# Pairwise dots of a DLRM tower: one wide matmul for four samples, against four narrow ones on their own array columns

## The reference

```python
e = jnp.stack([tbl_0[ids[:, 0]], ..., tbl_26[ids[:, 26]]], axis=1)   # (2048, 27, 128)
dot = jnp.einsum('bnd,bmd->bnm', e, e)
z = dot.reshape(2048, 27 * 27)[:, idx]          # the 351 pairs i < j
h = jnp.concatenate([z, dense_ctx], axis=1)     # 351 + 16 columns
h = jnp.maximum(h @ W_top1 + b_top1, 0.0)       # 367 -> 512
h = jnp.maximum(h @ W_top2 + b_top2, 0.0)       # 512 -> 256
y = h @ W_top3                                  # 256 -> 1
```

## Time and profile before

| | us |
|---|---|
| median of 2 runs | 441.38 |
| the two runs | 442.3 and 440.45 |
| span of the profiled execution | 599.8 |

### The profile page before, as it was taken

How to read it: one execution, slowest core, us unless ns; L and a number is a source line. 1 busy time by engine, 2 the same in 40 slices (tenths; PEclk the granted TensorE clock), 3 DMA queues, 4 the chain that set the end, 5 groups by cost and what they waited for, 6 DMA issues and landing times.

```text
span 599.8 us, 8311 instructions
## 1 busy us (share of the span) xinstructions
PE 416.3 (69%) x2864; PEld 391.5 (65%) x2864; DVE 263.6 (44%) x723; ACT 169.1 (28%) x296; POOL 291.1 (49%) x311
## 2 busy tenths in 40 slices
PE   2130749647876887689766986598768966998607
PEld 2120648647876876688666985597768856998506
DVE  5210745354636444435427462563536453642302
ACT  2110304213323242223223332243323231444201
POOL 6775543645665456545664566545655656000000
PEclk9755667768878998779976987699769987998957
DMA  7941211211341133212431234113321333012230
GB/s 199 248 124 44 68 44 49 80 36 54 96 128 43 37 99 102 79 32 75 99 106 29 70 84 120 43 28 98 102 76 35 92 95 96 4 49 59 50 38 11
DMA packets 58896, 45.29 MB, mean 76 GB/s; under 512 B 39972, under 2 KB 52644, under 8 KB 58876
## 3 DMA queue, kind: packets, MB, share of 16 engines
q1 hardware_dynamic: 49148, 25.09, 16.6%
q0 software_dynamic: 9728, 19.94, 12.4%
HBM read 37.92 MB, written 7.09 MB: 75 GB/s over the span
## 4 chain that ended last, share of the span: by engine, by line
PE 37%; another core or an unknown queue 31%; issue 9%; DVE 9%; DMA 8%; ACT 4%; SPq 1%; ACTq 0%; DVEq 0%
PE dots_ps L605 12%; PE onehot_ps L581 6%; DMA dots_dram<-dots 6%; DVE mask L486 6%; PE onehot_ps L583 6%; PE tile_ps L594 4%; PE mlp_ps L614 3%; PE mlp_ps L616 3%; PE mlp_ps L615 3%; ACT emb L366 2%; DVE dots L204 2%; ACT dots L204 1%; DVE tab_lo L505 1%; DMA emb<-tbl 1%
## 5 line engine op out<-in xcount | busy, mean ns | idle before, releaser
L344 POOL DMA_INDIRECT rows<-tbl,idx x304 | 290.4, 955 | 218.1 <-issue 102.8
L581 PE MATMUL onehot_ps<-mask,tab_hi 125*128 125x256 f32 x512 | 159.5, 338 | 85.0 <-DVE mask L486 43.3
L486 DVE TENSOR_SCALAR mask<-idb,cmp 125x256 fp32r<-125x256 int32 x512 | 155.4, 372 | 85.7 <-remote 59.0
L581 PEld LDWEIGHTS onehot_ps<-mask,tab_hi 125*128 125x128 f32 x512 | 119.2, 233 | 91.1 <-issue 62.7
L605 PE MATMUL dots_ps<-emb 128*128 128x108 f32 x1024 | 145.3, 300 | 30.7 <-ACT emb L366 20.3
L605 PEld LDWEIGHTS dots_ps<-emb 128*128 128x128 f32 x1024 | 138.5, 215 | 38.6 <-issue 26.9
L204 DVE COPY dots<-dots_ps 32x216 f32<-32x216 f32 x128 | 66.8, 522 | 207.9 <-remote 127.8
L583 PE MATMUL onehot_ps<-mask,tab_lo 125*128 125x256 f32 x512 | 151.1, 321 | 2.0 <-issue 2.0
L583 PEld LDWEIGHTS onehot_ps<-mask,tab_lo 125*128 125x128 f32 x512 | 119.4, 233 | 0.8 <-issue 0.7
L204 ACT COPY dots<-dots_ps 32x216 f32<-32x216 f32 x128 | 67.1, 524 | 165.3 <-remote 88.7
L594 PE MATMUL tile_ps<-ident,rows 128*128 128x128 f32 x304 | 56.7, 313 | 37.0 <-ACT emb L366 27.2
(11 more groups left out here) (32 smaller groups left out, 150.2 us busy)
## 6 DMA issues: line engine op xcount, KB each, us to landing
idb<-ids_onehot SPq DMA_DIRECT2D x16, 512.0 KB
dots_dram<-dots SPq DMA_DIRECT2D x7, 864.0 KB
rows<-tbl,idx POOLq DMA_INDIRECT x304
emb<-tbl SPq DMA_DIRECT2D x8, 448.0 KB
zT<-dots_dram SPq DMA_DIRECT2D x16, 117.0 KB
idb<-ids_onehot SPq DMA_DIRECT2D x8, 128.0 KB, 4.3
zT<-dots_dram SPq DMA_DIRECT2D x8, 104.0 KB
dots_dram<-dots SPq DMA_DIRECT2D x1, 540.0 KB
```

What stands on the lines that cost most here:

```text
L344: nc.gpsimd.indirect_dma_start(rows[:, q, r, :], None, tables[GATHERED[r]][:, :], bass.IndirectOffsetOnAxis(idx[:, k, r:r + 1], 0)).then_i ...
L486: made = nc.vector.tensor_scalar(mask[0:VP, h, c, :], idb[0:VP, f, :], cmp[0:VP, at:at + 1], None, ALU.is_equal)
L581: nc.tensor.matmul(out, tab_hi[0:VP, f, at, :], mask[0:VP, h, c, :], start=(at == 0), stop=False)
```

## The change

For each sample of a quad there is now a matmul of its own: 32 columns of weights (the sample's), 27 columns streamed, with the output on the 32 partitions of that sample, which puts it on its own 32 columns of the array. All 8 quads of a unit lie side by side in one bank (8 x 27 = 216 columns). Each engine then empties its two samples, which are 64 neighbouring partitions, in one copy.

```diff
 def empty_dots(copy, engine, b, parity, u, samples, empty):
     engine.wait_ge(dots_ps_full, UNITS * b + u + 1)
-    for s in samples:
-        a, z = PAD * s, PAD * (s + 1)
-        src = dots_ps[a:z, u % 2, :, 0:QUADS_BANK * QUAD * FEATURES].rearrange(
-            "p a (c t j) -> p a c t j", c=QUADS_BANK, t=QUAD)[:, :, :, s, :]
-        dst = dots[a:z, parity, :, u * UNIT_Q:(u + 1) * UNIT_Q].rearrange(
-            "p j (a c) -> p a c j", a=UNIT_BANKS)
-        taken = copy(dst, src)
-    taken.then_inc(empty, 1)
+    a, z = PAD * samples[0], PAD * (samples[-1] + 1)
+    copy(dots[a:z, parity, :, u * UNIT_Q:(u + 1) * UNIT_Q],
+         dots_ps[a:z, u % 2, 0, 0:UNIT_Q * FEATURES].rearrange("p (c j) -> p j c", c=UNIT_Q)
+         ).then_inc(empty, 1)
...
 def dot_unit(b, parity, u):
...
     for i in range(UNIT_Q):
-        at = (u * UNIT_Q + i) * QUAD
-        col = i % QUADS_BANK * QUAD * FEATURES
-        done = nc.tensor.matmul(
-            dots_ps[:, u % 2, i // QUADS_BANK, col:col + QUAD * FEATURES].rearrange(
-                "p (t j) -> p t j", t=QUAD),
-            emb[:, parity, at:at + QUAD, :], emb[:, parity, at:at + QUAD, 0:FEATURES],
-            start=True, stop=True)
+        for s in range(QUAD):
+            at = (u * UNIT_Q + i) * QUAD + s
+            done = nc.tensor.matmul(
+                dots_ps[PAD * s:PAD * (s + 1), u % 2, 0, i * FEATURES:(i + 1) * FEATURES],
+                emb[:, parity, at, :], emb[:, parity, at, 0:FEATURES], start=True, stop=True)
     done.then_inc(dots_ps_full, 1)
```

## The result

The changed kernel takes 457.87 us (456.94 and 458.8) against 441.38: 1.0386 times the time before, 95% interval 1.0346 to 1.0427 (the two medians by themselves divide to 1.037). The forecast was 441. It is slower by 3.9%, and yet PE has less to do.

The account below looks back on a forecast made before the run. POOL's gathers were taken to bound the kernel: 382 + 2.5 + 55.0 = 439.5 us, near the measured 441.38. With PE's extra work hidden and 0.5 us saved at the end, the forecast was 441 us, range 430 to 510.

Parts of the forecast that it names:

- POOL bounds the kernel: Whole kernel: POOL's 304 gathers, 1.245 us apart, set the time, and PE has 28 us of slack.
- the rebuilt 439.5 us: Undisturbed time of the kernel before, from POOL's durations: 382 + 2.5 + 55.0 us, against a median of 441.38.
- POOL, SP, the stores. Untouched: Gathers, waits on transposes, dots layout and DMAs stay the same, with gathers still 1.245 us apart.
- the forecast's own case: Narrow pairs cost 7 to 32 ns, all hidden under POOL: 441 us, range 434 to 449, chance 0.56.
- Copies ... Nothing of that is on the path: Dots copies on VectorE and ScalarE: one of 0.52 us replaces two, saving 0.52 us a unit, off the path.
- Matmuls: PE's dots: 64 narrow pairs at 28 to 30 ns make 1.86 us a unit, almost the 1.77 of before.
- rival A: Narrow pairs in dot_unit cost over 31 ns, so PE bounds: 457 us at 35 ns, 514 at 50; chance 0.25.
- Array switches: PE, each unit of dots: going into narrow weights and out again costs 0.26 us, bounds 0 and 0.3.
- B: PE's longer loop body has its instructions fetched again: 36 more packets, up to 29 us, 463 us; chance 0.06.
- C: Narrow matmuls bring PE a colder clock: about 560 us if 1.2 GHz holds half the time; chance 0.05.
- D: Recorder slowed POOL too, PE with its copies is the bound: about 400 us, or 415 with waits; chance 0.08.
- The end of the kernel: Last four units of dots taken as unchanged; the shorter last copy, ahead of the last store, saves 0.5 us.

Follow-up runs that it names:

- e2: Changed kernel with its narrow matmuls, but each engine copying 32 partitions twice, features innermost, as in the kernel before: 439.63 us, 0.9967 of the kernel before.
- e3: Changed kernel with the 16 wide matmul instructions put back, keeping one copy of 64 partitions per engine: 458.11 us, 1.0373 of the kernel before.
- e8: Changed kernel with VectorE making two copies of 32 partitions, quads innermost, and ScalarE one new copy: 439.16 us, 0.9964 of the kernel before.

## Why the prediction was wrong, point by point

- **POOL bounds the kernel: right.** The chain of the second profile of before is 52% POOL, its span is 439.0, and the stops of the earlier trace rows are not in it, so they were of that one profile. It stayed right after the change: POOL's excess is the loss. That the rebuilt 439.5 us met the span so well is partly luck. The last gather ended at 385.9 and not at 382, its landing took 4.0 us and not 2.5, and the rest took 49.1 in place of 55.0; the misses cancel.
- **"POOL, SP, the stores. Untouched": the step that failed.** The instructions and waits of POOL were untouched, its durations not. I took 1.245 us from start to start as a constant of the gather. It is one only as long as VectorE leaves gaps. 20.6 us were missing in this term, and the range of the forecast's own case (434 to 449) had nothing for it.
- **"Copies ... Nothing of that is on the path": failed with it.** The copy is off the path by its own time, and acts on it by the stream of VectorE's work that it joins to the masks. The size missed as well: 0.37 and 0.33 us against the 0.52 taken, at the lower bound of 0.36 and a little under it. I had asked what the shorter copies save, and not what follows behind them on VectorE.
- **Matmuls: the direction was wrong, harmlessly.** A unit of 64 pairs was taken as 1.86 us at 29 ns a pair. The timeline of after:

```profile
300.32 0.28 PE L580 MATMUL onehot_ps<-mask,tab_lo 125*128 125x256 f32 x1
300.53 0.75 PE L603 MATMUL dots_ps<-emb 128*32 128x27 f32 x64
301.24 0.64 PE L591 MATMUL tile_ps<-ident,rows 128*128 128x128 f32 x4
```

  Without the length of the last one (0.19) the starts of 64 pairs spread over 0.56 us, 8.9 ns apart. The lower bound, four column groups side by side (7 ns), was nearly the true one. This is one of the shortest units; half of the 64 spread over 0.78 us or more. The unit with its switches takes 301.24 - 300.53 = 0.71 us and 0.09 of entry, 1.0 us less than the 1.77 of the earlier trace rows and not 0.35 more. The figure of some 25 ns, quoted from the Trainium skill beside rival A (TensorE: Matmul & The Clock Gate, section Back-to-back issue gap), does not hold for neighbours on different column groups.
- **Array switches: right in size.** From the last one-hot the first dots follow after 0.21 us instead of 0.12, and the transposes start 0.15 us after the last dots: 0.24 us in and out together, against 0.26 taken.
- **Rival A (dear pair) fell** with the pair. **B:** 52 packets came, against 48 worked out, but e2 has all 52 at 0.9967: they hold nothing up. **C:** the granted clock fell, 0.865 against 0.957, but e2 runs at 0.903 without a loss and e3, with the wide matmul, at 0.937 with all of it. **D** had PE as the bound, and it is not: an easier PE gave no time, except at the end. (Its 400 us did not follow from its own saving of 52 either, which gives 389.)
- **The end of the kernel: right in sign, too small.** -0.5 us was forecast for the last copy. From the last gather's start to the end it is 4.8 us less. The last units of dots take 415.57 - 410.40 = 5.2 us, where they took 9.02 in the earlier trace rows and 8.9 in the second profile, and VectorE's work from there to the last store 0.4 us in place of 2.7; the store itself took 3.3 us more. The chain of waits of after, in order of time (start, length, what):

```profile
402.01 5.02 DMA rows<-tbl,idx
...
410.40 3.42 PE dots_ps L603 x239
413.82 1.27 issue
415.09 0.48 PE dots_ps L603 x17
415.60 0.39 DVE dots L200
416.00 20.84 DMA dots_dram<-dots
```

- No rival was this one. The range reached to 510 for A's sake, so it held 457.87, but by luck, for another reason than the one given.

## What to carry to other kernels

Where GpSimd issues indirect DMAs all the time, their rate is not a constant: write down with it what VectorE does meanwhile, and treat every edit that shortens or joins VectorE's work as one that may close the gaps that the gathers go on in. Look for gathers of two and three times the usual length and lay VectorE's timeline beside them before anything else. Here the narrow matmuls are free and safe with VectorE's two old copies (0.9967 and 0.9978), or with all copies on ScalarE (0.9961 [0.9937, 0.9985], the lowest ratio, not to be told from e8's 0.9964); a lighter PE pays next to nothing while gathers bound the kernel.

## What the runs showed of the hardware that was not expected

- A gather of 0.94 us can be held for about 2 us by eight VectorE instructions of 0.262 us spacing, though in other tables it is let in between two of them: VectorE then loses 0.1 to 0.2 us, and the gather hardly anything.
- Whether VectorE's instructions had run dry just ahead of the masks sorts the tables: 1 held of 530 where they had, 118 of 382 where the first mask began before the last instruction ended.
- Narrow matmuls (32 columns of weights, 27 streamed) on four column groups start 8.9 ns apart in the shortest units (0.56 us for 64).
- A copy of 32 partitions and one of 64 take the same time (367 and 370 ns on VectorE with quads innermost), and one of 128 takes 340 on ScalarE where 64 take 334. With the features innermost the same 216 numbers take 524 to 534 ns.
